# Windowed attention inside one adaLN block: causal masks in 32-row pieces, V projected once per token, plain output transposes, a new order on VectorE, ScalarE and TensorE

## The reference

```python
qkv = x @ w_qkv; q, k, v = split into 16 heads of 8
kcat, vcat = concat(previous chunk, own chunk)          # 2 * 64 keys
scores = einsum(qc, kcat) / sqrt(8)
mask = (wq + 64 >= jk) & (ci * 64 + jk - 64 >= 0)       # causal; chunk 0 has no previous chunk
out = softmax(where(mask, scores, -inf)) @ vcat
x = x + ga * (out @ w_out)
h = layernorm(x) * (1 + cb) + sb
x = x + gb * sum over the 2 best experts of weight * (silu(h @ W1.T) * (h @ W3.T)) @ W2.T
```

## Time and profile before

| | us |
|---|---|
| median of 3 runs (lowest 273.75, highest 278.57) | 276.14 |
| the profiled execution | 275.3 |
| its span, first to last instruction | 273.1 |
| attention stage, to the last `scores_t` | about 141 |
| expert stage and the final sums | about 132 |

### The profile page before, as it was taken

How to read it: one execution, slowest core, us unless ns; L and a number is a source line. 1 busy time by engine, 2 the same in 40 slices (tenths; PEclk the granted TensorE clock), 3 DMA queues, 4 the chain that set the end, 5 groups by cost and what they waited for, 6 DMA issues and landing times.

```text
span 273.1 us, 7726 instructions
## 1 busy us (share of the span) xinstructions
PE 218.6 (80%) x2696; PEld 149.7 (55%) x2698; DVE 166.8 (61%) x527; ACT 115.3 (42%) x259; POOL 126.6 (46%) x125
## 2 busy tenths in 40 slices
PE   6875998999989899997688875698999999993000
PEld 2442465756546575664456654476778887872000
DVE  4695599998585968858472944633444444442492
ACT  3324455546554544654435331223444444433430
POOL 5727263508549183764224174523444444444251
PEclk9999799999999999999979995979999999999555
DMA  6329900000000010000101121231121111100851
GB/s 185 108 79 431 447 23 2 4 2 22 22 13 29 2 33 12 22 22 13 31 22 58 31 60 48 69 88 59 58 60 57 48 52 43 58 21 31 265 159 38
DMA packets 16488, 19.32 MB, mean 71 GB/s; under 512 B 2578, under 2 KB 14998, under 8 KB 16202
## 3 DMA queue, kind: packets, MB, share of 16 engines
q1 hardware_dynamic: 13786, 14.43, 16.6%
q0 software_dynamic: 2240, 4.28, 4.5%
q10 hardware_dynamic: 432, 0.20, 0.3%
HBM read 13.03 MB, written 6.13 MB: 70 GB/s over the span
## 4 chain that ended last, share of the span: by engine, by line
PE 59%; DVE 16%; DMA 6%; ACT 6%; issue 4%; another core or an unknown queue 2%; POOL 2%; SPq 1%; ACTq 0%; DVEq 0%; POOLq 0%
PE pair L754 9%; PE pair L728 7%; PE pair L730 7%; PE pair L560 4%; PE pair L539 4%; DVE nd L1010 4%; ACT pt L841 4%; PE pair L736 4%; PE pair L504 4%; PE pair L545 3%; PE pair L575 3%; PE pair L476 2%; DVE fin_b L1330 2%; PE pair L534 2%
## 5 line engine op out<-in xcount | busy, mean ns | idle before, releaser
L1440 POOL DMA_INDIRECT ranked<-y_sb,ix_u x36 | 35.4, 984 | 46.5 <-ACT y_sb L930 35.9
L1306 DVE TENSOR_TENSOR gated<-pair,act 128x352 f32<-128x352 f32 x36 | 18.9, 524 | 51.8 <-PE pair L730 41.8
L841 ACT ACTIVATE pt<-pair 128x1024 f32<-128x1024 f32 x32 | 33.0, 1030 | 31.7 <-PE pair L545 31.7
L1010 DVE TENSOR_REDUCE nd<-pair 128x8 f32<-128x1024 f32 x32 | 37.7, 1220 | 9.4 <-PE pair L504 9.1
L1392 POOL DMA_INDIRECT routed<-pay,row_u x32 | 32.4, 1012 | 12.6 <-issue 6.3
L754 PE MATMUL pair<-we_sb,gated_t 128*128 x216 | 31.9, 286 | 0.8 <-ACT y_sb L930 0.8
L728 PE MATMUL pair<-we_sb,x_t 128*128 x72 | 29.7, 495 | 2.8 <-ACT x_t L924 2.8
L754 PEld LDWEIGHTS pair<-we_sb,gated_t 128*128 128x128 f32 x216 | 28.2, 199 | 1.7 <-issue 1.6
L730 PE MATMUL pair<-we_sb,x_t 128*128 x72 | 28.2, 474 | 0.0
L1357 POOL TENSOR_TENSOR rstd<-veps,cf_sb 128x2 f32<-128x2 f32 x8 | 6.0, 748 | 47.5 <-DVE veps L1050 47.5
L914 ACT ACTIVATE act<-pair 128x352 f32<-128x352 f32 x36 | 16.7, 464 | 16.0 <-PE pair L728 16.0
(11 more groups left out here) (167 smaller groups left out, 388.1 us busy)
## 6 DMA issues: line engine op xcount, KB each, us to landing
we_sb<-we SPq DMA_DIRECT2D x1, 4352.0 KB, 18.9
xt_in<-routed SPq DMA_DIRECT2D x36, 64.5 KB
mod_bc<-mod_rows SPq DMA_DIRECT2D x1, 2048.0 KB, 8.7
fin_y<-ranked SPq DMA_DIRECT2D x8, 256.0 KB, 4.7
out<-fin_b SPq DMA_DIRECT2D x8, 128.0 KB, 1.8
x_all<-x SPq DMA_DIRECT2D x1, 768.0 KB, 6.2
ranked<-y_sb,ix_u POOLq DMA_INDIRECT x36
routed<-pay,row_u POOLq DMA_INDIRECT x32
```

The lines of the kernel that those rows point to most:

```text
L841: act.activation(pt[:, 2 * half:2 * half + 2, :].rearrange("p j k -> p (j k)"), src[:, :], ACT.Exp).then_inc(done, 1)
L1010: dve.tensor_reduce(nd[:, :, 2 * half:2 * half + 2, 0].rearrange("p s j -> p j s"), src[:, :].rearrange("p (j s k) -> p j s k", j=2, s=4), ...
L1440: pool.indirect_dma_start(ranked[:, :], bass.IndirectOffsetOnAxis(ap=ix_u[q][:, 0:1], axis=0), y_sb[q][:, :], None, bounds_check=TOPK * TO ...
```

## The change

- The masks are kept in `late32` (128 x 96, bfloat16), loaded by 8 small DMAs on SP between `cb_sb` and the second part of `x_all`. In `scores` 16 matmuls with 32x32 weights take the place of 8 (two for each a and bank: 32 queries with 256 columns, the other 32 with 128). In `scores_t` 8 matmuls take the place of 4: four with 32x64 weights and 256 columns, then four with 32x32 weights and 256 columns. TensorE and VectorE wait for all 9 loads (`ld_b`, 144).
- `project_v` makes two matmuls; `copy_v` makes three copies, two of which move 64 partitions to the other half. `h_t` loses its 64 zero columns.
- `output_t` is four plain transposes of 128 columns; `perm_o` goes. `divide_output` reads 16 x 2 x 8 values with a stride.
- TensorE: `gate(b-2)` moves from after scores_t(2b) to before project_v, into M1 (Z1 at b = 8), `prefix(b-2)` from before out_project to after scores_t(2b+1), into M1. project_v and the gate wait for `negt_ready`.
- ScalarE: both exponentials come before the copy of the maxima.
- VectorE: in `period0(b)` the order is neg_max, norm_stats, norm, read_gate, choose_experts, and divide_output last (first of the gate's work at b = 8). `read_gate` also waits for `v_copied` of the batch whose V lies in M1.

```diff
+            la = CB["late"][0]
+            for j in range(4):
+                sp.dma_start(late32[32 * j:32 * j + 32, 0:W], cb[0:32, la:la + W]).then_inc(ld_b, 16)
+                sp.dma_start(late32[32 * j:32 * j + 32, W:W + 32], cb[32:64, la + 32:la + W]).then_inc(ld_b, 16)
...
-                for c in range(4):
-                    last = mm(M1[:, c * P:(c + 1) * P], h_t[:, c * W:c * W + 2 * W], wqkv_sb[:, 2 * D:3 * D],
+                for t in range(2):
+                    last = mm(M1[:, t * P:(t + 1) * P], h_t[:, t * P:(t + 1) * P], wqkv_sb[:, 2 * D:3 * D],
...
+                for a in range(2):
+                    for j in range(4):
+                        sv = S_BANKS[j].rearrange("p (s k) -> p s k", s=4)
+                        one = group(ident_b, j)[:, 32 * j:32 * j + 32]
+                        mm(sv[64 * a:64 * a + 32, :, W:2 * W], one, group(late, j), start=True, stop=False,
+                           skip_group_check=True)
+                        mm(sv[64 * a + 32:64 * a + 64, :, W + 32:2 * W], one, group(later, j), start=True, stop=False,
+                           skip_group_check=True)
...
+                for j in range(4):
...
+                    mm(fv[64:128, :, 0:32], group(late32, j)[:, 0:W], one, start=False, stop=False,
+                       skip_group_check=True)
+                for j in range(4):
...
+                    last = mm(fv[96:128, :, 32:64], group(late32, j)[:, W:W + 32], one, start=False, stop=True,
+                              skip_group_check=True)
...
-                        last = mm(M0[:, at:at + RCOLS], o_sb[:, p, r, :], perm_o[:, :], start=True, stop=True,
-                                  skip_group_check=True)
+                        last = pe.transpose(M0[:, at:at + P], o_sb[:, p, r, :], ident)
...
+                if b < B:
+                    pe.wait_ge(negt_ready, 2 * b + 1)
+                if b >= 2:
+                    gate(b - 2, M1 if b < B else Z1)
                 if b + 1 < B:
-                    pe.wait_ge(negt_ready, 2 * b + 1)
                     project_v()
...
-                act.copy(v_lane[b % 2][:, :, HD:2 * HD],
-                         M1.rearrange("p (h e) -> p h e", e=HD)).then_inc(v_copied, 1)
+                act.copy(to[:, :, 1, :, :], v)
+                act.copy(to[W:2 * W, :, 0, :, :], v[0:W])
+                act.copy(to[0:W, 1, 0, :, :], v[W:2 * W, 0, :, :]).then_inc(v_copied, 1)
...
                     exp_to(2 * b, 0)
+                    exp_to(2 * b, 1)
                     copy_neg_max(2 * b + 1)
-                    exp_to(2 * b, 1)
...
-                if b >= 1:
-                    divide_output(b - 1)
-                if b >= 2:
-                    choose_experts(b - 2, M0)
                 if b == 0:
                     norm_stats(4, 4)
                 if b == 1:
                     norm_stats(12, 4)
                 if b + 2 < B:
                     norm(b + 2, 2 if b < 2 else 3 if b < 4 else 4)
+                if b == B:
+                    divide_output(b - 1)
+                if b >= 2:
+                    read_gate(b - 2, M1 if b < B else Z1)
+                    choose_experts(b - 2)
+                if 1 <= b < B:
+                    divide_output(b - 1)
```

More of the change, by code:

```diff
@@ L60 @@
 N_CB = _columns(CB, [("ident", P), ("before", P), ("ones", P), ("region", E), ("late", 4 * W), ("none", 4 * W)])
-CB_USED = CB["late"][0] + W
+CB_USED = CB["late"][0]
 def build(nc, x, c_t, wqkv, wout, wmod, wg_t, we, cf, cr, cb, out):
@@ L200, in group @@
             return t[32 * j:32 * j + 32]
-        def half(t, i):
-            return t[64 * i:64 * i + 64]
         def mod(b, which):
@@ L487, in scores @@
                     pe.wait_ge(max_y, g)
-                for n in range(2):
-                    for a in range(2):
-                        for i in range(2):
-                            sv = S_BANKS[2 * i + n].rearrange("p (s k) -> p s k", s=4)
-                            mm(half(sv, a)[:, :, W:2 * W], half(ident_b, i)[:, 64 * i:64 * i + 64],
-                               half(late, i).unsqueeze(1).to_broadcast([W, 4, W]), start=True, stop=False,
-                               skip_group_check=True)
+                late = late32[:, 0:W].unsqueeze(1).to_broadcast([P, 4, W])
+                later = late32[:, W:W + 32].unsqueeze(1).to_broadcast([P, 4, 32])
+                for a in range(2):
[6 more added lines that the diff above has]
+                           skip_group_check=True)
                 if g == 0:
@@ L503, in scores @@
                     for j in range(4):
-                        last = mm(half(S_BANKS[j], a), group(q_sb, j)[:, c * W:c * W + W],
+                        last = mm(S_BANKS[j][64 * a:64 * a + 64, :], group(q_sb, j)[:, c * W:c * W + W],
                                   group(km[par], j)[:, :, c * W:c * W + 2 * W], start=False, stop=True,
@@ L540, in scores_t @@
                            group(qm[par], j)[:, :, c * W:(c + 1) * W], start=False, stop=False, skip_group_check=True)
-                for n in range(2):
-                    for i in range(2):
-                        fv = F_BANKS[2 * i + n].rearrange("p (s q) -> p s q", s=8)
-                        one = half(ident_b, i)[:, 64 * i:64 * i + 64].unsqueeze(1).to_broadcast([W, 8, W])
-                        last = mm(half(fv, 1), half(late, i), one, start=False, stop=True, skip_group_check=True)
+                for j in range(4):
+                    one = group(ident_b, j)[:, 32 * j:32 * j + 32].unsqueeze(1).to_broadcast([32, 8, 32])
+                    fv = F_BANKS[j].rearrange("p (s q) -> p s q", s=8)
+                    mm(fv[64:128, :, 0:32], group(late32, j)[:, 0:W], one, start=False, stop=False,
+                       skip_group_check=True)
+                for j in range(4):
+                    one = group(ident_b, j)[:, 32 * j:32 * j + 32].unsqueeze(1).to_broadcast([32, 8, 32])
+                    fv = F_BANKS[j].rearrange("p (s q) -> p s q", s=8)
+                    last = mm(fv[96:128, :, 32:64], group(late32, j)[:, W:W + 32], one, start=False, stop=True,
+                              skip_group_check=True)
                 last.then_inc(f_done, 1)
@@ L646, in period0 @@
                     pe.wait_ge(x2_ready, b - 1)
-                    gate(b - 2, M0)
                 if b >= 1:
@@ L666, in period1 @@
                 pv(2 * b)
-                if b >= 2:
-                    pe.wait_ge(sc8_ready, b - 1)
-                    prefix(b - 2, M0)
                 if b >= 1:
@@ L1227, in period1 @@
                 if b >= 2:
-                    place_rows(b - 2, M0)
+                    place_rows(b - 2, M1)
                 if b >= 1:
@@ L1272, in aside @@
                 if i == 5 and at == "b":
-                    choose_experts(B - 1, XT_BANK)
+                    read_gate(B - 1, XT_BANK)
+                    choose_experts(B - 1)
                 if i == 6:
```

68 lines of the change are left out of this document (34 added, 34 removed).

## The result

The changed kernel takes **283.96 us** (median of 5 runs, 283.45 to 286.79) against 274.68 us before (5 runs, 273.75 to 278.57): ratio **1.0363**, 95% interval 1.0314 to 1.0412. It is slower, where 272.3 us and "no change" had been forecast. The profiled execution took 286.79 us (span 284.9) against 275.3 (span 273.1). Medians here are over all executions of a kernel, a ratio and its 95% interval are formed from those without its slower, lower-clocked executions, so the two can differ. The profiled execution of the changed kernel is the longest of its five, 2.8 us above the median, so its rows show a little more than the loss of the medians.

A forecast was written before the change was run, and what follows sets the result against it. TensorE was taken as close to its bound in the steady iterations, with two waits to remove. Prologue -0.4, b = 1 and 2 +0.8, steady iterations -3.6, b = 7 -0.6 gave -3.8: 276.14 to 272.3 us, range 268.2 to 275.8.

The forecast's parts named there:

- part 2 of the sum: Steady iteration, from the masks of scores_t(2b) to scores_t(2b+1): 6.48 us was to become 5.44, saving 1.04.
- part 1: Steady iteration, from the odd exponential to the masks of scores_t(2b): 7.71 us was to become 7.94.
- part 3: Steady iteration, from scores_t(2b+1) to its exponential: 1.88 us was to become 1.78 through a shorter last mask round.
- the last rival: choose_experts runs into `qm` on VectorE, delaying division and on_transpose; +0.43 us per steady iteration on before, 277.7 us; 8%.
- The exponential: Even group's exponential of X, steady iteration: start moves from m + 0.99 to m + 0.89 with the shorter last mask round.
- b = 1 and 2: Early iterations: norm and gate work ahead of the division delay scores_t, less 0.10 of masks each; sum +0.8 us.
- Masks: Steady iteration, TensorE: masks of scores_t 0.47 us for 0.55, masks of scores 0.30 for 0.34.
- The steady batch: Iterations b = 3 to 6: 16.07 us was to become 15.16, -0.91 each, -3.6 over four.
- Prologue: Stretch up to b = 1: shorter project_v and masks were to gain 0.4 us, if the small loads land in time.
- b = 7: Last iteration before the expert stage: choice ahead of the division starts VectorE's table work earlier, -0.6 us.
- The order at the port: Rival in b = 1 or 2: L1014 starts ahead of `km`; one turn gives 270.8 us, two 269.3; 20%.
- the instruction supply: Rival: 22 more matmuls per iteration bring a 0.35 us issue gap in each of five, +1.75, 274 us; 20%.

The follow-up runs named there:

- b_qm_first: The kernel before with GpSimd's mask_q ahead of the scatters of tile (b-3, 1), nothing else; ratio 0.9961.
- b_gate_split: The kernel before with GpSimd edits alone: km waits for the negated maxima, qm earlier, the scatters of tile (b-3, 1) set apart; 271.69 us, 1.0005.
- a_choice_pool: The changed kernel with choice of experts and norm behind the division, and GpSimd's qm ahead of the scatters; 272.69 us, ratio 0.9923.
- a_choice_last: The changed kernel with the choice of experts behind the division again and the norm last; 275.64 us, ratio 1.0009.
- sets 2 and 4: Runs of single parts, and of scatters placed where nothing waits, each set on one chip; the kernel before took 268.93 and 269.02 us there.
- sets 1 and 3: Runs on the two stalls, and on the port order set by a wait, each set on one chip; the kernel before took 275.32 and 274.61 us.
- before_again: The kernel before, unchanged, traced again on a fifth chip; ratio 1.0024.
- a_qm_first: The changed kernel with GpSimd's mask_q(b+1) ahead of the scatters of tile (b-3, 1); 279.39 us, ratio 1.0097.
- a_scatter_pair: The changed kernel with the choice behind the division and both tiles scattered together at the end of GpSimd's list; 271.00 us, ratio 1.018.

## Why the prediction was wrong

**The step that failed is part 2 of the sum, from m to scores_t(2b+1).** In b = 5, at the full clock, part 1 took 8.00 us for 7.94 and part 3 1.79 for 1.78, but part 2 took 7.05 for 5.44. Both terms that should have been out of the way there were wrong. (m is the start of the masks of scores_t(2b), here 108.89.) The exponential of X was put at m + 0.89 and started at m + 2.50. The division was put at m + 2.55 with a slack of 0.75 and ended at m + 4.80. So on_transpose, put at m + 3.31, started at m + 4.92. One of the two I had as a rival, the other not at all.

**The division: the condition of the last rival failed, and with it its 8%.** The mechanism, the place (the choice's last additions on `qm`) and the sign were named, and the rival's times came true: division at m + 4.6, on_transpose at m + 4.65. I let it decide "if they are 0.25 late", because `qm` started at km + 2.44 and the choice was to end at km + 2.19. The choice was on time: hot_b started at km's end + 1.88. But the port was taken before `qm`'s recorded start. In b = 3 to 5 hot_b began 0.57 or 0.58 us ahead of it, beside the second scatter, in b = 6 hot_2 0.53 ahead, and each was held to the end of `qm`. hot, 0.23 earlier, was free. No lateness was needed; a slack of 0.25 read between two starts was none. Whether the scatter or `qm` took it is open. The Trainium skill (SBUF — State Buffer, "Who interferes with whom") says that issue order decides who blocks, and of VectorE's two-port modes that whoever issues first has the shared pair for the whole instruction while the other fully blocks. Held whole is what the trace shows, but by recorded starts VectorE had issued first and was blocked all the same.

**Its price was mis-sized.** I had +0.43 a batch on before, 277.7 us in all. At the full clock the batch was +0.77 and +0.71 (b = 5 and 6), the late exponential included, and I left out what a longer idle time of TensorE does to its clock: about 4.3 us.

**The exponential: a term was missing.** I took the idle 1.49 us of the even exponential in the earlier trace rows for the pace of TensorE. It is 0.33 us longer than in b = 2 (1.16), because of the scatters (b_qm_first: 1.16 in every batch once they are elsewhere). In the changed kernel the lateness became 2 us, which by itself brings TensorE to on_transpose at m + 4.92 in b = 5, held division or not. The two hide each other there: by these rows, taking away one alone would leave the other. Wherever an edit puts the scatters, what is late moves with them: exp X, the reduce, the copy of on_t, pv.

**b = 1 and 2** were to cost 0.8 and cost 0.75 + 1.68. Missing is a wait that the change adds and I did not price: neg_max_t(5) stood still behind read_gate, which stood behind norm and the held subtraction. The kernel before has no such wait ahead of this neg_max_t.

```profile
56.00 0.38 PE L513 MATMUL pair<-cb_sb,nd 128*128 128x128 bf16 x4 [1.44 <-DVE sc L1087]
```

It takes scores(6) with it, and the clock falls there too (0.90 over the batch).

**The rest, by its steps.** V: 0.65 for 1.09, right. Masks: 0.45 in scores_t and 0.26 in scores, for 0.47 and 0.30, right; measured at 0.27 a batch. The copies of V (0.37, 0.36, 0.26) lie ahead of the exponential, right. ScalarE's order: nothing, right. The steady batch was to fall by 0.91; with the stalls edited away it falls by 0.95 on one chip (against b_gate_split). That the sum fits this so well is in part luck, since b_gate_split's batch is 15.27, not 16.07. Prologue -0.4: -0.3 here, but this stretch varied between 28.3 and 33.1 us over the runs, so it can't be told. b = 7, -0.6: 16.65 for 16.60 (VectorE's table work starts 11.1 us behind the odd exponential of b = 6 for 11.4, but on_transpose waits 1.77 for the division), and the expert stage did not stay as long as it was (+2.6). The order at the port (20%) did not turn in the changed kernel (L1021 starts 6 ns behind `km` in b = 2 and is held) but did in a_choice_pool in the same batch, where it starts 5 ns behind and is free, for 0.7 us (14.22, against 14.91 in a_choice_last, where it is held). Of the instruction supply (20%), a part is true that I had not meant: TensorE stops without a wait beside scatters, with or without the change's extra matmuls.

**What stays open.** Why a scatter disturbs TensorE, and why on some chips only. On the chips of sets 2 and 4 no exponential or reduce was over 0.4 us late beside scatters, on those of sets 1 and 3 up to 1.8 us. The reduce of the odd group shows it with the same code around it: 0.74 to 0.80 us behind the scores' end in the first trace of before and in before_again, 0.17 in b_gate_split. The trace also records when each semaphore was raised. TensorE's are raised 0.01 to 0.09 us behind the modelled end where no scatter is near. In b = 3 of the changed kernel the masks, output_t and neg_max_t end at 71.61, 72.20 and 72.42, and their semaphores are raised at 73.65, 73.70 and 73.76, closer together than the work between them takes; in b = 4 of a_choice_pool scores and on_transpose end at 84.96 and 85.33 and are announced at 86.19 and 86.23. That speaks for messages that are held and then let go together. The gaps inside pv show that TensorE's own instructions are held up too. What holds either is not shown. Leaving the scatters out altogether was not tried. How to make the table earlier, which now bounds a faster attention stage, was not tried either.

## What to carry to other kernels

Read the distance between a VectorE instruction with two SBUF inputs and the next GpSimd instruction as a risk from both sides: with a scatter ahead of it in GpSimd's queue, the port was gone 0.5 us before the recorded start, and whatever stands behind the held instruction (here the division) should have been ahead of it. Before reordering an in-order engine, list what now waits behind its longest possible hold, and price TensorE's idle time with the clock it may lose. And measure an edit on more than one chip: one version was 2.8% faster on one and no faster on another (1.0045, 1.0 to 1.009). A faster first stage is worth only what the second can take up: here TensorE then stood 3.6 us before its first expert tile, on both chips.

## What was not expected of the hardware

- A scatter issued by GpSimd (DMA_INDIRECT, about 1 us) makes consumers of TensorE's results start late on three of five chips, by up to 1.8 us (reduce) and 2 us (exponential), and cuts a run of matmuls without waits (gaps of 0.35 and 0.41 us marked "issue"). `km` and `qm`, longer GpSimd instructions, do not: beside `qm` the exponential waits 0.63 (a_qm_first).
- Whether VectorE's small subtraction is held by `km` isn't settled by the recorded starts: 5 ns behind it was free in a_choice_pool and held in a_scatter_pair, 6 ns behind held, 50 ns ahead free, 130 ns ahead held for 4.35 us.
- An idle gap of TensorE of 2.2 us left the clock at 1.00 in b = 5. Gaps of 2.3 and 2.2 us in b = 3 and 4 were followed by stretches at 0.50.
- Five chips fell into two groups: 268.9 and 269.0 us for the kernel before, or 274.5 to 275.3.
